# Exponentials and side counts of a pair of score groups moved one pair later or earlier in an attention pipeline

## What is computed

```python
q, k = l2norm(x @ Wq), l2norm(x @ Wk)                 # 16 heads of 64; 4 memory keys ahead of the 512
dots = einsum('bhid,bhjd->bhij', q, k) * 10
dots = einsum('hg,bgij->bhij', W_pre_th, dots)        # heads are mixed
dots = where(causal, mask_value, dots)
vk   = top_k(dots, 64)[0][..., -1:]                   # 64th largest of each row
dots = where(dots < vk, mask_value, dots)
attn = softmax(dots); attn = einsum('hg,bgij->bhij', W_post_th, attn)
out  = einsum('bhij,bhjd->bhid', attn, v) * head_scale * sigmoid(x @ Wg + bg)
x    = x + out @ Wo
```

## Time and profile before

| | |
|---|---|
| median of 3 runs | 3655.68 us (3652.28 to 3657.66) |
| the profiled execution | 3655.08 us, its span 3653.3 us |
| busy share of the span: PE, DVE, ACT, POOL | 71%, 52%, 51%, 39% |
| mean granted clock of TensorE, share of full speed | 0.795 |

### The profile page before, as it was taken

One profiled execution on the slowest core, in us unless ns is written; L12 is line 12 of the kernel. 1 busy time (PEld: TensorE's weight loads), 2 busy tenths in 40 slices (PEclk: granted clock), 3 DMA queues, 4 the chain that ended last, 5 costly groups with the idle time before them and its releaser, 6 DMA issues. The chain is left out here.

```text
span 3653.3 us, 58885 instructions
## 1 busy us (share of the span) xinstructions
PE 2599.6 (71%) x16099; PEld 1681.3 (46%) x16100; DVE 1887.3 (52%) x7291; ACT 1875.9 (51%) x6078; POOL 1442.4 (39%) x3918
## 2 busy tenths in 40 slices
PE   1985777777777776767677777676777777766498
PEld 1433444544454445544454445443544455444333
DVE  4262555545563556355545555455645563567335
ACT  1433555555654555455545554556545554565143
POOL 2003544444344444454444444544444335443000
PEclk9997777777877777877787777778877877787599
DMA  3001011001010111011101010011001010111101
GB/s 112 0 17 42 19 33 45 10 22 34 22 26 19 29 36 28 16 28 39 26 13 31 23 44 11 22 34 45 10 22 33 20 28 16 28 38 26 54 0 46
DMA packets 112976, 104.77 MB, mean 29 GB/s; under 512 B 34192, under 2 KB 110608, under 8 KB 112656
## 3 DMA queue, kind: packets, MB, share of 16 engines
q1 hardware_dynamic: 107744, 96.64, 10.4%
q10 hardware_dynamic: 4912, 4.46, 0.4%
HBM read 19.13 MB, written 12.71 MB: 9 GB/s over the span
## 5 line engine op out<-in xcount | busy, mean ns | idle before, releaser
L1395 DVE SCALAR_TENSOR_TENSOR E<-S,limit,E 128x68 f32<-128x68 f32 (+56 forms) x456 | 248.8, 579 | 1099.9 <-ACT E L1077 1074.3
L859 PE MATMUL bankC<-R,E 128*128 128x128 f32 x2560 | 475.4, 340 | 414.7 <-POOL R L1228 414.4
L859 PEld LDWEIGHTS bankC<-R,E 128*128 128x128 f32 x2560 | 415.0, 240 | 523.5 <-POOL R L1228 500.4
L1087 ACT COPY PT<-bankC 128x512 f32<-128x512 f32 (+3 forms) x512 | 216.5, 424 | 594.4 <-PE bankC L859 586.3
L1217 POOL TENSOR_SCALAR est<-below 128x1 f32<-128x1 f32 x456 | 93.2, 205 | 1029.0 <-ACT junk L1061 1007.7
L835 PE MATMUL bankD<-KT,QT 64*64 64x258 f32 (+7 forms) x2304 | 236.1, 485 | 353.2 <-ACT SC L1036 319.4
L845 PE MATMUL bankB<-raw,mixpre 128*128 128x76 f32 (+37 forms) x1024 | 417.7, 497 | 6.3 <-DMA raw<-SC 5.4
L1069 ACT ACTIVATE junk<-S 128x68 bf16<-128x68 f32 (+56 forms) x456 | 199.7, 439 | 432.3 <-DVE S L1333 432.0
L884 PE MATMUL bankM<-PT,V 128*64 128x64 f32 x5120 | 311.7, 292 | 0.8 <-ACT PTtail L1092 0.8
L845 PEld LDWEIGHTS bankB<-raw,mixpre 128*128 128x128 f32 x1024 | 187.6, 220 | 207.0 <-issue 188.0
L1189 POOL TENSOR_TENSOR S<-S,diagmask 128x8 f32<-128x8 f32 x512 | 127.3, 255 | 389.8 <-ACT S L1050 324.2
(11 more groups left out here) (173 smaller groups left out, 5428.5 us busy)
## 6 DMA issues: line engine op xcount, KB each, us to landing
X_first<-in_L_attn_x_dram ACTq DMA_DIRECT2D x8, 512.0 KB, 10.1
x<-X_first SPq DMA_DIRECT2D x8, 512.0 KB, 4.7
xt<-x SPq DMA_DIRECT2D x32, 128.0 KB, 3.2
x<-xt SPq DMA_DIRECT2D x32, 128.0 KB, 2.5
X_last<-x SPq DMA_DIRECT2D x8, 512.0 KB, 6.7
out_dram<-X_last SPq DMA_DIRECT2D x8, 512.0 KB, 3.2
raw<-SC SPq DMA_DIRECT2D x8, 258.0 KB, 4.5
raw<-SC SPq DMA_DIRECT2D x8, 254.0 KB, 4.1
```

The costliest lines, as they stand in the source:

```text
L859: last = nc.tensor.matmul(bankC[n % 2][:, jb * P:(jb + 1) * P], E[n % 4][:, jb * P:(jb + 1) * P], R[n % 2][:, :], start=True, stop=True)
L1087: last = nc.scalar.copy(PT[u % 2][:, 0:blocks, :, at:at + IG], bankC[n % 2][:, 0:blocks * P].rearrange("p (j h i) -> p j h i", h=H, i=IG))
L1395: at[n] = step(nc.vector.scalar_tensor_tensor(out=E[n % 4][:, 0:w], in0=S[n % SBUFS][:, 0:w], scalar=least, in1=E[n % 4][:, 0:w], op0=ALU. ...
```

## The change

Line numbers of rows taken before are those of the old code; the new code stands 3 to 4 lines lower up to the POOL loop, and from L1360 on 1 to 3 lines off.

- **ACT, pass n0:** the side counts are those of pair n0-4 (they were of pair n0-2), the exponentials those of pair n0-4 (they were of pair n0-6). Both stand together behind evict(n0+1), side counts first, and both `out_PT` behind them.
- **DVE, `select_pair(n0)`:** shift and row maxima stand at its end, and are those of pair n0+4 (they stood in its middle, of pair n0+2). Four row maxima instead of two are taken ahead of the loop.
- **POOL, pass n0:** nmax comes first, then scaled_mix, then second_threshold; nmax was last, second_threshold first.
- `ln_stats` of tile t+2 goes from g = 6 to g = 4; the second `squares` of a tile (L1300, feeding the k half of `norm`) goes from g = 14 of one tile to g = 0 of the next, one position later on DVE.
- Two waits of ACT on itself are added, and two waits' counts changed, for the order in which `junk` is written. No instruction is added or taken away, no size changes, and SP's queue and PE's order are the same.

```diff
--- before.py
+++ after.py
@@ -1043,6 +1043,8 @@
                 if is_ranked(n):
                     if ranked_upto(n - 2):
                         act.wait_ge(below_done, ranked_upto(n - 2))
+                    if ranked_upto(n - 6):
+                        act.wait_ge(signs_done, ranked_upto(n - 6))
                     nc.scalar.activation(junk[n % 2][:, 0:wide(n)], src, ACT.Square, scale=wide(n) ** -0.5,
                                          accum_out=msq[:, col(n)]).then_inc(summed, 1)
                     if is_wide(n):
@@ -1054,8 +1056,8 @@
 
             def count_below(n):
                 act.wait_ge(thr0_ready, ranked_upto(n))
-                if ranked_upto(n - 2):
-                    act.wait_ge(signs_done, ranked_upto(n - 2))
+                if ranked_upto(n - 4):
+                    act.wait_ge(signs_done, ranked_upto(n - 4))
                 act.wait_ge(summed, ranked_upto(n))
                 w = group_width(n)
                 nc.scalar.activation(junk[n % 2][:, 0:w], S[n % SBUFS][:, 0:w], ACT.Sign, scale=-1.0,
@@ -1063,8 +1065,10 @@
 
             def count_sides(n):
                 act.wait_ge(shifted, ranked_upto(n))
-                act.wait_ge(summed, ranked_upto(min(n + 2, NG - 1)))
-                act.wait_ge(below_done, ranked_upto(n))
+                if ranked_upto(n - 2):
+                    act.wait_ge(signs_done, ranked_upto(n - 2))
+                act.wait_ge(summed, ranked_upto(min(n + 4, NG - 1)))
+                act.wait_ge(below_done, ranked_upto(min(n + 2, NG - 1)))
                 w = group_width(n)
                 nc.scalar.activation(junk[n % 2][:, 0:w], S[n % SBUFS][:, 0:w], ACT.Sign,
                                      accum_out=signs[:, col(n)]).then_inc(signs_done, 1)
@@ -1126,16 +1130,15 @@
                         score(2 * t + 2, 1)
                     if g == 14 and ahead:
                         score(2 * t + 2, 3)
-                for n in (n0 - 6, n0 - 5):
+                if live:
+                    evict(n0 + 1)
+                for n in ranked_in(n0 - 4):
+                    count_sides(n)
+                for n in (n0 - 4, n0 - 3):
                     if 0 <= n < NG:
                         exp(n)
-                if live:
-                    evict(n0 + 1)
                 if n0 >= LAG:
                     out_PT(n0 - LAG)
-                for n in ranked_in(n0 - 2):
-                    count_sides(n)
-                if n0 >= LAG:
                     out_PT(n0 + 1 - LAG)
                 if live:
                     if g == 0 and ahead:
@@ -1236,21 +1239,21 @@
             for n0 in range(0, NG + LAG, 2):
                 t, g = divmod(n0, GPT)
                 live, ahead = n0 < NG, t + 1 < NT
-                if ranked_in(n0 - 2):
-                    second_threshold(ranked_in(n0 - 2))
+                if 0 <= n0 - 4 < NG:
+                    m = n0 - 4
+                    pool.wait_ge(max_done, m + 2)
+                    nc.gpsimd.tensor_scalar(nmax[:, ring((m, m + 1))], rmax[:, ring((m, m + 1))], -1.0, 1.0, ALU.mult,
+                                            ALU.mult).then_inc(nmax_ready, 2)
                 if n0 >= LAG:
                     scaled_mix(n0 - LAG)
                     scaled_mix(n0 + 1 - LAG)
+                if ranked_in(n0 - 2):
+                    second_threshold(ranked_in(n0 - 2))
                 if live:
                     mask(n0)
                     mask(n0 + 1)
                     if ranked_in(n0):
                         first_threshold(ranked_in(n0))
-                if 0 <= n0 - 4 < NG:
-                    m = n0 - 4
-                    pool.wait_ge(max_done, m + 2)
-                    nc.gpsimd.tensor_scalar(nmax[:, ring((m, m + 1))], rmax[:, ring((m, m + 1))], -1.0, 1.0, ALU.mult,
-                                            ALU.mult).then_inc(nmax_ready, 2)
                 for m in (n0 - 4, n0 - 3):
                     if 0 <= m < NG and m % GPB < 4:
                         if m >= 4:
@@ -1358,8 +1361,6 @@
                     for n in ranked:
                         dve.wait_ge(tk, at[n])
                         at[n] = step(nc.vector.max(top[n % 2][:, 0:8], near[n % 2][:, 0:group_width(n)]))
-                for n in ranked_in(n0 + 2):
-                    shift(n)
                 for r in range(1, WINDOW // 8):
                     for n in ranked:
                         row = near[n % 2][:, 0:group_width(n)]
@@ -1369,9 +1370,6 @@
                     for n in ranked:
                         dve.wait_ge(tk, at[n])
                         at[n] = step(nc.vector.max(top[n % 2][:, 8 * r:8 * r + 8], near[n % 2][:, 0:group_width(n)]))
-                if n0 + 2 < NG:
-                    for n in (n0 + 2, n0 + 3):
-                        row_max(n, ranked_upto(n))
                 if ranked:
                     for n in ranked:
                         dve.wait_ge(tk, max(at[n], ordered))
@@ -1397,6 +1395,11 @@
                         op0=ALU.is_ge, op1=ALU.mult, accum_out=rsum[:, col(n)]))
                 dve.wait_ge(tk, at[n0 + 1])
                 nc.vector.reciprocal(rinv[:, ring(both)], rsum[:, ring(both)]).then_inc(E_ready, 2)
+                for n in ranked_in(n0 + 4):
+                    shift(n)
+                if n0 + 4 < NG:
+                    for n in (n0 + 4, n0 + 5):
+                        row_max(n, ranked_upto(n))
 
             def mark_batch(i):
 
@@ -1416,13 +1419,13 @@
             squares(0, 1)
             ln_stats(1)
             ln_apply(1)
-            for n in range(2):
+            for n in range(4):
                 row_max(n, 0)
             squares(1, 0)
             squares(1, 1)
             for n0 in range(0, NG, 2):
                 t, g = divmod(n0, GPT)
-                if g == 6 and t + 2 < NT:
+                if g == 4 and t + 2 < NT:
                     ln_stats(t + 2)
                 select_pair(n0)
                 if g == 4 and t:
@@ -1436,8 +1439,8 @@
                     if t + 2 < NT:
                         squares(t + 2, 0)
                     gate_half(2 * t)
-                if g == 14 and t + 2 < NT:
-                    squares(t + 2, 1)
+                if g == 0 and t and t + 1 < NT:
+                    squares(t + 1, 1)
                 if (n0 + 2) % GPB == 0:
                     mark_batch(n0 // GPB)
             gate_half(NU - 1)
```

## The result

| | before | after |
|---|---|---|
| median | 3654.6 us | **3030.6 us** (3029.7 to 3033.3) |
| span of the profiled execution | 3653.3 | 3027.9 |
| PE busy in the span | 2599.6 | 2380.2 |
| PE idle in the span | 1053.7 | 647.7 |
| mean granted clock | 0.795 | 0.857 |

The ratio is 0.829, with a 95% interval of 0.828 to 0.831: 17% less time. 3170 us had been forecast, with a range from 3060 to 3410.

A forecast was written before the change was run, and what follows sets the result against it. Two circles of waits, ACT with DVE, and POOL's R behind second_threshold needing ACT's counts, were taken to bound the kernel. 245 + 190 + 53 - 30 + 30 = 488 us off 3655 gave 3170 us, range 3060 to 3410.

The forecast's parts named there:

- Part 1: ACT's side counts, DVE's shift and maxima: ACT's wait for the shift leaves PE's gaps ahead of score copies; 245 us saved.
- part 4: ACT's exponentials behind PE's turns: an exponential and both PT copies then follow an attend; 30 us lost.
- Parts 2 and 3: POOL: nmax and R ahead of second_threshold end PE's waits for R, 190 us; the norm-of-k gap shortens, 53 us.
- Part 5: PE's granted clock: matmuls behind shortened gaps return to full clock; 30 us taken, from 0 to 205.
- ScalarE did not become the pace: Rival on ACT: PE's wait for R only turns into a wait for score copies; 3360 us, chance 0.25.
- part 2: POOL: with nmax and R ahead of second_threshold, PE's waits for R go except those behind norm; 190 us saved.
- DVE did not fall behind: Rival on DVE: its circle closes through E, each attend putting a pair's work on the path; about 3900 us, chance 0.04.
- The clock pays more: Rival on PE's clock: the two wait savings as forecast and all 205 us of clock instead of 30; 2990 us, chance 0.12.
- The sign set for a term too small: PE's mean clock of 0.85 or more would mean the clock term of 30 us was too small.
- the sign for part 1: ACT's side counts would wait for DVE under 50 us in all.
- Four others: PE's SC waits about 100 us; R waits nearly all g = 8; ACT's exponentials wait only g = 0, 8; DVE's longest: exponentials.
- The rule against the change: POOL's R may be held by DVE's two-input multiply: 239 us more if every R took 836 ns; charged nothing.

The follow-up runs named there:

- e1: The kernel before with one edit: R (scaled_mix) ahead of second_threshold on POOL, all else as it was; 3442.3 us, ratio 0.941.
- e4: The kernel before, order untouched, with matmuls that nothing reads filling PE's gaps; 3575.4 us, ratio 0.978.
- e3: The changed kernel with the norm of k on POOL moved from the end of pass g = 6 to behind R in pass g = 8; 2800.6 us, ratio 0.767.
- e2: The changed kernel with one edit undone: second_threshold ahead of R again on POOL, nmax still first; 3385.1 us, ratio 0.927.

## Why the prediction was wrong

The direction and the mechanism of the waits came as forecast, the time did not: 3030.6 us lies 140 under the forecast and 30 under the range.

- **Part 1, 245 us less 30 of part 4.** Waits for the score copies and the k piece fell by 375.3 - 197.4 = 178 us. The pass that was worked out in detail came within 0.1 us. The forecast for both parts was 215, so some 37 us were missing. Besides, PE's waits for the DMA of `raw` grew by 37 us in the faster passes, which no part had.
- **Parts 2 and 3, 190 + 53 = 243 us.** Waits for R fell by 242.6, but that the sum fits is luck twice over. Counted by pass, the waits at g = 8, behind the norm, fell from 200 to 119 us, 81 against 53; all others from 215 to 53, 162 against 190. And e1 shows that this number holds only with the other circle open too: alone, the same edit gave back 118 of its 231 us as other waits. The terms were summed as if each stood for itself, and the sum came out only because the change opens both.
- **All idle terms together:** 458 us forecast, 406 measured. They were 52 us too large and do not explain a time below the range.
- **Part 5, the clock: this is the step that failed.** It was put at 30 us of 0 to 205 and measured 219. Two things were wrong in its working. First, its upper bound counted one mix pair and one score behind each of 80 gaps, and the attends; but half clock lasted longer than these, and the gaps ahead of g = 0 and the other waits for R were not in it. The rows by line of the two kernels show where the time came back. Mix and score, the two that were counted, gave 60 us of their 110; the attends 26, of which 23 at g = 0. Matmuls that no term had gave most of the rest: the turns (L859) 54 us, the k projection (L795) 30, the output projection (L899) 29. e4 found 433 us to be had. Second, inside the range it was put near the bottom because "the passes stay uneven". The prediction's own numbers spoke against that: the ten gaps were forecast to shrink to 13.2 us together, 1.3 us each. With 219 in place of 30 the forecast would have been 3655 - 458 - 219 = 2978; the 52 us of idle time too many give the 3030 measured. One row in front of the forecast showed that half clock goes on beyond a mix and a score: the k projection behind a gap of 2.17 us took 6.25, and one tile earlier, with next to no gap ahead, 3.67:

```profile
1470.22 3.67 PE L795 MATMUL bankD<-Wk,xnT 128*128 128x512 f32 x8 [0.31 <-ACT SC L1036]
```

- **The attends** stayed at half clock, as part 5 had it, because the norm's gap stayed. The 95 us put on them were well judged: with that gap gone, e3 has them 90 us shorter.
- **The rivals.** ScalarE did not become the pace: PE's waits for its copies fell by 178 us where that rival had them take over the 190 of part 2. DVE did not fall behind: its longest wait is 356.3 us ahead of the shift, for POOL's threshold. "The clock pays more" is the case that came, at 3031 instead of 2990, and it had been given 0.12 because its price was tied to the attends.
- **What would show it.** The sign set for a term too small, a mean clock of 0.85 or more, came: 0.857. ACT's waits for the shift went, as the sign for part 1 had it. Four others failed, wholly or in part. PE's waits for SC are 158.8 us, not about 100. Of its 171.8 us for R, 119 are at g = 8 and 37 at g = 4 and 6, not nearly all at g = 8. ACT waits ahead of its exponentials outside g = 0 and g = 8: 76 us at g = 12, where the output projection stands between the turns; the PT copies had waited 85 us there before. And DVE waits longest for the threshold, not for the exponentials; it has slack for that.
- **The rule against the change.** R takes 367 ns in the median and at most 805, as before, and POOL's busy time went from 1442.4 to 1446.2 us: nothing, as counted. The contention shows on another line, as told in the last section.

What stays open: why R comes so much later in e2, whose 105 us of added waits for it make up most of what only both halves of the change bring.

## What to carry to other kernels

When PE stops and goes, add up its busy time by granted clock before pricing an edit that shortens its waits (here 1144 of 2600 us at half clock): the idle time is one gain, and matmuls that come back from half clock are a second, here half as large as the first. Filling gaps with matmuls that nothing reads measures that store in one run, if the filling is timed by a row of its own size and stays shorter than the gaps. In engines that run in program order, let what one hands to the other stand a whole pass away, in every queue that it passes; one of two such circles opened alone gives less than its part.

## What was not expected of the hardware

A VectorE instruction with two inputs in SBUF can be held by one of GpSimd for as long as that runs. The `limit` operation of DVE works on two columns and never took more than 0.20 us before. In the changed kernel 15 of its 232 instances start while POOL runs the product of the norm (1.90 us), and these take 1.81 us on average (views of the line, ns: least, median, most; before and after):

```profile
L1383 DVE TENSOR_TENSOR limit<-key,flip x232: 158/160/201, 364.0 to 3376.3; 128x2 int32<-128x2 int32 x112, 128x1 int32<-128x1 int32 x4
L1381 DVE TENSOR_TENSOR limit<-key,flip x232: 158/161/1842, 359.8 to 2752.0; 128x2 int32<-128x2 int32 x112, 128x1 int32<-128x1 int32 x4
```

The multiply into E meets the same product. Here 380 columns took 2.14 us beside it, and the next, eight columns wider, 0.61:

```profile
1459.49 1.90 POOL L1186 TENSOR_TENSOR qk<-qk,rn 128x1024 f32<-128x1024 f32 x1
...
1459.66 2.14 DVE L1393 SCALAR_TENSOR_TENSOR E<-S,limit,E 128x380 f32<-128x380 f32 x1
...
1461.73 0.61 DVE L1393 SCALAR_TENSOR_TENSOR E<-S,limit,E 128x388 f32<-128x388 f32 x1
```

This is not new with the change: 23 of these multiplies started inside such a product before, the longest 2.08 us, and 7 do after. The Trainium skill, page "SBUF — State Buffer", section "Who interferes with whom", says that a VectorE instruction with two SBUF inputs contends with a GpSimd instruction that reads SBUF, that the port pair they share is an exclusive lock, and that the order of issue decides who blocks. The trace agrees: the DVE instruction came second and ended behind POOL's, `limit` by 0.02 us and the multiply of 380 columns by 0.41. The prediction had looked for the cost on R; it is on DVE. DVE's busy time rose by 54 us in all (1887.3 to 1941.4), 26 of them on `limit`, while the multiplies took 10 us less; none of it is known to have reached the end.

And the share of the attend's time that is clock is not one half. Twelve matmuls of the attend took 0.91 us at 0.50 and 0.57 at 1.00, the whole attend 9.3 and 5.8: full clock gives back 38% of it.
